# Large side items of TensorE cut in two pieces and issued from a queue with a share for each unit of scores

## What is computed

```python
x = x + 0.5 * ffn(layernorm(x))
x = x + attn(layernorm(x))
x = x + 0.5 * ffn(layernorm(x))
# attn: 16 heads of 16; k and q normalised per head, scaled by 256 ** -0.25
dot = where(causal, -inf, q @ k.T); out = softmax(dot) @ v; out @ Wo.T + bo
# ffn: base + shared low-rank + routed low-rank (6 experts of rank 16, 2 taken)
base_out = x @ base_W.T + base_b
shared_out = (x @ shared_A.T) @ shared_B.T
gate = softmax(x @ router_W.T + router_b); two largest, normalised, others 0
routed_out = sum over e of gate[e] * (x @ routed_A[e].T) @ routed_B[e].T
```

## Time and profile before

| | us |
|---|---|
| median of 3 runs | 1363.42 |
| lowest and highest run | 1358.17, 1364.6 |
| profiled execution | 1358.05 |
| its span, first to last instruction | 1356.3 |
| TensorE busy in it | 1164.8 |
| ScalarE busy in it | 1021.1 |
| VectorE busy in it | 458.1 |
| GpSimd busy in it | 232.9 |
| mean granted TensorE clock | 0.958 |

### The profile page before, as it was taken

The page is one execution under the profiler, slowest core; times in us unless marked ns, Lnnn a source line. Parts: engine busy times, 40 slices in busy tenths (PEclk is TensorE's granted clock), DMA queues, the critical chain, the costliest instruction groups (busy, mean ns, idle before and its releaser), DMA issues.

```text
span 1356.3 us, 23146 instructions
## 1 busy us (share of the span) xinstructions
PE 1164.8 (86%) x9076; PEld 382.2 (28%) x9076; DVE 458.1 (34%) x1164; ACT 1021.1 (75%) x1132; POOL 232.9 (17%) x377
## 2 busy tenths in 40 slices
PE   2636877889889998999989998999999999999984
PEld 2522432323323232232322222222222222121222
DVE  4655537356444533443234232122222011010114
ACT  2203555567677878788888997899999999999960
POOL 2223432222222122211022002102102001000000
PEclk9768898999999999999999999999999999999996
DMA  4011200300210021000200001100001100000000
GB/s 129 1 55 32 72 1 26 85 0 2 74 37 2 1 77 35 1 1 17 74 23 1 1 1 56 40 1 1 1 1 47 49 2 1 0 1 1 9 9 16
DMA packets 39673, 33.39 MB, mean 25 GB/s; under 512 B 8786, under 2 KB 39496, under 8 KB 39560
## 3 DMA queue, kind: packets, MB, share of 16 engines
q1 hardware_dynamic: 37360, 31.74, 8.0%
q10 hardware_dynamic: 2200, 0.12, 0.1%
HBM read 18.73 MB, written 12.85 MB: 23 GB/s over the span
## 4 chain that ended last, share of the span: by engine, by line
PE 61%; ACT 14%; DVE 11%; issue 8%; POOL 1%; DMA 1%; SPq 1%; ACTq 1%; DVEq 0%; POOLq 0%
PE ps L1088 56%; ACT ring L695 14%; PE ps L1127 2%; PE ps L1188 1%; DVE oT L1068 1%; DVE xnT L767 1%; DMA x<-in_x 1%; PE ps L1296 1%; DVE st L726 1%; SPq L527 1%; PE ps L1304 1%; PE ps L1147 1%; DVE xnT L765 1%; DVE area L747 1%; DVE att L1075 1%
## 5 line engine op out<-in xcount | busy, mean ns | idle before, releaser
L695 ACT ACTIVATE ring<-ps 128x1024 f32<-128x1024 f32 x1056 | 989.7, 1107 | 178.5 <-PE ps L1088 175.8
L1088 PE MATMUL ps<-ring,vf 128*17 128x512 f32 (+3 forms) x4608 | 566.0, 569 | 2.9 <-POOL ring L649 2.0
L1088 PE MATMUL ps<-queries,keys 50*128 50x512 f16 (+3 forms) x2304 | 380.4, 371 | 34.3 <-DMA queries<-shift_d 9.9
L1088 PEld LDWEIGHTS ps<-queries,keys 50*128 50x128 f16 x2304 | 93.5, 93 | 504.1 <-ACT ring L695 425.5
L649 POOL TENSOR_SCALAR_AFFINE_SELECT ring<-ring 128x256 f32<-128x256 f32 (+1 forms) x224 | 95.6, 443 | 434.0 <-ACT ring L695 432.9
L1088 PEld LDWEIGHTS ps<-ring,vf 128*17 128x17 f32 x4608 | 80.1, 96 | 173.5 <-issue 148.1
L765 DVE CAST xnT<-ps 128x512 f16<-128x512 f32 x50 | 34.5, 691 | 160.8 <-PE ps L1127 115.4
L1068 DVE COPY oT<-ps 128x512 f32<-128x512 f32 x32 | 22.1, 690 | 165.9 <-PE ps L1088 165.6
L899 DVE SCALAR_TENSOR_TENSOR x<-ps,power,x 128x512 f32<-128x512 f32 x32 | 24.0, 750 | 124.2 <-PE ps L1088 124.2
L461 POOL TENSOR_TENSOR sq<-area 128x512 f32<-128x512 f32 x32 | 33.7, 1052 | 184.4 <-DVE ss L904 89.7
L1088 PE MATMUL ps<-baseT,xnT 128*128 128x256 f16 x384 | 56.6, 287 | 8.1 <-DVE qT L932 2.7
(11 more groups left out here) (145 smaller groups left out, 703.7 us busy)
## 6 DMA issues: line engine op xcount, KB each, us to landing
parts_d<-split SPq DMA_DIRECT2D x32, 256.0 KB, 2.6
keys<-parts_d SPq DMA_DIRECT2D x96, 64.0 KB, 2.3
queries<-parts_d SPq DMA_DIRECT2D x192, 32.0 KB
x<-in_x SPq DMA_DIRECT2D x8, 512.0 KB, 3.9
out_x<-x SPq DMA_DIRECT2D x16, 256.0 KB, 2.2
queries<-shift_d SPq DMA_DIRECT2D x64, 4.0 KB
ring<-in_base_W SPq DMA_DIRECT2D x1, 256.0 KB, 4.6
ring<-in_Wq SPq DMA_DIRECT2D x1, 256.0 KB, 5.8
```

Source lines behind the costliest of these rows:

```text
L695: act.activation(probs[:, u % RING, :], bank(2 * (u % SLOTS), 2), ACTF.Exp, bias=0.0, scale=1.0).then_inc(exp_ok, 1)
L1088: return pe.matmul(o, lhsT, rhs, start=start, stop=stop, skip_group_check=True)
```

## The change

The side items of a unit are no longer issued at once. They are appended to a queue, and from it a unit issues items while the sum of their new weights (`PIECES`) stays within `SHARE`, 0.85. The first item of a unit is issued whatever it weighs, and steps that TensorE has no part in weigh 0. The queue is emptied whole 8 units and 3 units ahead of a chunk's end and at the last unit.

`inner`, `outer`, `qk`, `value` and `projout` become two entries in the queue: `("half", item)` for the first half of the matmuls, and the item itself for the second. Only the second signals that the bank is ready, and only the first waits for the bank. The other engines have no step named `half` and pass over it; they take their part at the second entry. When a `divide` is due and a first half is outstanding, its second half is issued ahead of it, since both use the same bank. At the start of the kernel both halves stand next to each other; the tail of chunk 7 isn't cut.

```diff
+
+PIECES = {"inner0": (2, 0.7), "inner1": (2, 0.7), "outer0": (2, 1.0), "outer1": (2, 1.0), "qk": (2, 0.75), "value": (2, 0.8), "projout": (2, 0.8),
+          "turn0": (1, 0.7), "turn1": (1, 0.7), "turn2": (1, 0.7), "turnin0": (1, 0.7), "turnin1": (1, 0.7), "turnout": (1, 0.7), "heads": (1, 0.7)}
+SHARE = 0.85
...
+def pieces(items):
+
+    for stage, n in items:
+        count, weight = PIECES.get(stage, (1, 0.0))
+        if count == 2:
+            yield weight, "half", (stage, n)
+        yield weight, stage, n
...
 def schedule():
     yield from startup()
-    for stage, n in together(prepare(0), front(0, 0, 1)):
+    for _, stage, n in pieces(together(prepare(0), front(0, 0, 1))):
         yield stage, n
...
-    values, groups, scored, split = [], [], set(), set()
+    values, groups, scored, split, queue, stage = [], [], set(), set(), deque(), None
...
         if groups and groups[0][0] <= u:
+            if stage == "half":
+
+                yield queue.popleft()[1:]
+                stage = None
             yield "divide", groups.pop(0)[1]
...
-        for stage, n in side[u]:
+        queue.extend(pieces(side[u]))
+        spent, flush = 0.0, u + 8 in UNIT0 or u + 3 in UNIT0 or u == NU - 1
+        while queue and (flush or not spent or spent + queue[0][0] <= SHARE):
+            w, stage, n = queue.popleft()
+            spent += w
             yield stage, n
...
+            def inner(K, f, c, halves=BOTH):
                 key = (f"inner{f}", c)
-                b = side_bank(K, key)
+                b = side_bank(K, key) if 0 in halves else bank(K.bank[key])
                 pe.wait_ge(K.w_ok, 1)
-                for a in range(2):
+                for a in halves:
                     pe.wait_ge(*K.done[f"turn{2 * f}", (c, a)])
-                for i in range(TC):
+                for i in (2 * a + k for a in halves for k in range(2)):
                     for ib in range(2):
                         m = mm_parts(b[:, i * NA:(i + 1) * NA], lambda s: xnT[2 * f][:, s, ib, i * P:(i + 1) * P], lambda s: aT[:, s, ib, :],
                                      i == 0 and ib == 0, i == TC - 1 and ib == 1)
-                m.then_inc(K.ready, 1)
+                if 1 in halves:
+                    m.then_inc(K.ready, 1)
...
-            def outer(K, f, c, a):
+            def outer(K, f, c, a, halves=BOTH):
                 key = (f"outer{f}", (c, a))
-                b = side_bank(K, key)
+                b = side_bank(K, key) if 0 in halves else bank(K.bank[key])
                 pe.wait_ge(K.w_ok, 3)
                 pe.wait_ge(*K.done[f"turnin{f}", c])
-                for i in range(2):
+                for i in halves:
                     t = slice((2 * a + i) * P, (2 * a + i + 1) * P)
                     o = b[:, i * D:(i + 1) * D]
                     for ib in range(2):
                         mm_parts(o, lambda s: xnT[2 * f][:, s, ib, t], lambda s: baseT[:, s, ib, :], i == 0 and ib == 0, False)
                     m = mm_parts(o, lambda s: hT[f][:, s, t], lambda s: bT[:, s, :], False, i == 1)
-                m.then_inc(K.ready, 1)
-
-            def project(K, n):
+                if 1 in halves:
+                    m.then_inc(K.ready, 1)
+
+            def project(K, n, halves=BOTH):
                 c, t = n // TC, slice(n % TC * P, (n % TC + 1) * P)
-                b = side_bank(K, ("qk", n))
+                b = side_bank(K, ("qk", n)) if 0 in halves else bank(K.bank["qk", n])
                 pe.wait_ge(K.w_ok, 5)
                 for i in range(2):
                     pe.wait_ge(*K.done["turn1", (c, i)])
-                for ib in range(2):
+                for ib in halves:
                     m = mm_parts(b, lambda s: xnT[1][:, s, ib, t], lambda s: qkT[:, s, ib, :], ib == 0, ib == 1)
-                m.then_inc(K.ready, 1)
-
-            def value(K, c, a):
-                b = side_bank(K, ("value", (c, a)))
+                if 1 in halves:
+                    m.then_inc(K.ready, 1)
+
+            def value(K, c, a, halves=BOTH):
+                b = side_bank(K, ("value", (c, a))) if 0 in halves else bank(K.bank["value", (c, a)])
                 pe.wait_ge(K.w_ok, 6)
                 for i in range(2):
                     pe.wait_ge(*K.done["turn1", (c, i)])
-                for i in range(2):
+                for i in halves:
                     for ib in range(2):
                         m = mm_parts(b[:, i * D:(i + 1) * D], lambda s: xnT[1][:, s, ib, (2 * a + i) * P:(2 * a + i + 1) * P],
                                      lambda s: vT[:, s, ib, :], i == 0 and ib == 0, i == 1 and ib == 1)
-                m.then_inc(K.ready, 1)
+                if 1 in halves:
+                    m.then_inc(K.ready, 1)
...
+            def project_out(c, a, halves):
+                key = ("projout", (c, a))
+                b = side_bank(main, key) if 0 in halves else bank(main.bank[key])
+                pe.wait_ge(*main.done["turnout", (c, a)])
+                for i in halves:
+                    for ib in range(2):
+                        m = mm_parts(b[:, i * D:(i + 1) * D], lambda s: xnT[2][:, s, ib, (2 * a + i) * P:(2 * a + i + 1) * P],
+                                     lambda s: woT[:, s, ib, :], i == 0 and ib == 0, i == 1 and ib == 1)
+                if 1 in halves:
+                    m.then_inc(main.ready, 1)
...
+            halved = None
             for stage, n in ORDER:
-                front_and_heads(main, stage, n)
+
+                if stage == "half":
+                    halved, halves = n, (0,)
+                    stage, n = n
+                else:
+                    halves = (1,) if (stage, n) == halved else BOTH
+                front_and_heads(main, stage, n, halves)
                 if stage == "scores":
                     scores(n)
...
-                    c, a = n
-                    b = side_bank(main, (stage, n))
-                    pe.wait_ge(*main.done["turnout", n])
-                    for i in range(2):
-                        for ib in range(2):
-                            m = mm_parts(b[:, i * D:(i + 1) * D], lambda s: xnT[2][:, s, ib, (2 * a + i) * P:(2 * a + i + 1) * P],
-                                         lambda s: woT[:, s, ib, :], i == 0 and ib == 0, i == 1 and ib == 1)
-                    m.then_inc(main.ready, 1)
+                    project_out(*n, halves)
```

More of the change, by code:

```diff
@@ L2 @@
 from concourse import mybir
+from collections import deque
 from contextlib import ExitStack
@@ L1128, in turn @@
                 m.then_inc(K.ready, 1)
-            def inner(K, f, c):
+            BOTH = (0, 1)
+            def inner(K, f, c, halves=BOTH):
                 key = (f"inner{f}", c)
-                b = side_bank(K, key)
+                b = side_bank(K, key) if 0 in halves else bank(K.bank[key])
                 pe.wait_ge(K.w_ok, 1)
-                for a in range(2):
+                for a in halves:
                     pe.wait_ge(*K.done[f"turn{2 * f}", (c, a)])
-                for i in range(TC):
+                for i in (2 * a + k for a in halves for k in range(2)):
                     for ib in range(2):
@@ L1189, in turn_heads, with front_and_heads @@
                 m.then_inc(K.ready, 1)
-            def front_and_heads(K, stage, n):
+            def front_and_heads(K, stage, n, halves=BOTH):
                 if stage == "weight":
@@ L1200, in front_and_heads @@
                 elif stage == "inner0":
-                    inner(K, 0, n)
+                    inner(K, 0, n, halves)
                 elif stage == "turnin0":
@@ L1204, in front_and_heads @@
                 elif stage == "outer0":
-                    outer(K, 0, *n)
+                    outer(K, 0, *n, halves=halves)
                 elif stage == "qk":
-                    project(K, n)
+                    project(K, n, halves)
                 elif stage == "value":
-                    value(K, *n)
+                    value(K, *n, halves)
                 elif stage == "heads":
                     turn_heads(K, *n)
+            def project_out(c, a, halves):
[8 more added lines that the diff above has]
+                    m.then_inc(main.ready, 1)
             pe.wait_ge(bnd, FLAG_STEPS)
@@ L1317, in _ @@
                 elif stage == "inner1":
-                    inner(main, 1, n)
+                    inner(main, 1, n, halves)
                 elif stage == "turnin1":
@@ L1321, in _ @@
                 elif stage == "outer1":
-                    outer(main, 1, *n)
+                    outer(main, 1, *n, halves)
 INPUTS = {
```

## The result

The kernel after takes 1389.46 us (median of 4 runs, 1388.80 to 1389.99), the kernel before 1361.75 beside it: a ratio of 1.0218, 95% interval 1.0193 to 1.0243. It is 2.2% slower. The forecast was 1348 us, 1327 to 1371, and faster.

The account below looks back on a forecast made before the run. ScalarE's wait for TensorE's scores, 175.8 us, was taken as the bound. Terms of -12.6, -1, -9, +6.6, -1, +2 and 0 gave -15.0 us: 1358.05 to 1343.0, then 5.4 up to a median of 1348, range 1327 to 1371.

Parts of the forecast that it names:

- (b): Chunks 2 to 6: 6 of 12 neighbour pairs sharing a unit are parted, saving bank wait and stall; 9 us gained.
- (a): Large items cut in two: 0.25 us gained an item in chunks 4 to 6, 0.1 in 2 and 3; 12.6 us.
- (c): Chunks 2 to 6: 11 more items start right behind another's end, each waiting 0.6 us for the bank; +6.6 us.
- a rival's reason: Rival of nothing measurable (1366 us, chance 0.20): side items share one bank, each holding it a unit longer.
- (d): Chunk 1: fewer items share a unit, more wait for the bank; net -1 us, ends -8 and +10.
- step (g): Work queued behind: VectorE and POOL steps come 0.3 to 0.4 units later in chunks 2 to 5, 2.2 in 1, unfelt.
- (e): Chunk 0: the flush at unit 12 makes a later but shorter burst, some 27 us; +2 us, ends -4 and +9.
- (f): Second pieces: their repeated semaphore waits are long satisfied and cost 0; at most 20 us for 95 pieces.
- The second rival: Chunks 0 and 1: the queue makes them a one-piece-a-unit chain, so slower by 11 us, 1374; chance 0.12.
- the 155 us: Mark of being right: ScalarE's wait for TensorE falls from 175.8 us to some 155.
- The wait of 2.25 us behind `heads` and `outer0`: Mark of being right: ScalarE's 2.25 us wait behind these two side items becomes about 1.
- (c)'s mark: Mark that the bank term is right: TensorE's waits for VectorE copies grow in number.

Follow-up runs that it names:

- e8: The changed kernel with items left whole and the queue only from chunk 2 on, chunks 0 and 1 in before's order; ratio to before .9992.
- e12: e8 with one unit left free behind each item's end; 1341.84 us, ratio to before .9865.
- e3: The changed kernel with the queue emptied in every unit of chunks 0 and 1, restoring before's order there; 1371.19 us, ratio to before 1.0091.
- e10: e3 with one unit left free behind each item's end from chunk 2 on; ratio to before .9924.
- e14: e12 with two free units instead of one behind an item's end from chunk 3 on; 1336.63 us, ratio to before .9826.
- e4: The kernel before, with every large item written as two entries next to each other, leaving only the repeated waits; ratio to before 1.0019.
- e1: The changed kernel with the queue and its flushes kept but no item cut; ratio to before 1.0027.

## Why the prediction was wrong

**What bounds the kernel** was read rightly: ScalarE waits for TensorE, chunks 0 and 1 are chains, and the single side bank is what pile-ups wait for. The sign of the cuts' term failed, and the gain under (b) did not come.

**(a) The cuts: -12.6 us; measured +8 to +13.5 us from chunk 2 on** (the table's columns). This is the step that failed. The flushes leave 92 of the 95 counted cuts parted. I took an item that stood alone, gave the first half its gain in full and returned half as a later stall. The runs show two costs that I had put at nothing. A cut costs TensorE .10 to .11 us: each half holds it for .76 us (300.51 to 301.27, 302.57 to 303.33), the whole for 1.40 (288.81 to 290.21), and so it is in all items from chunk 2 on. And it interrupts ScalarE's runs more often, 200 times instead of 135 in chunks 2 to 6, for .1 us each. A third is argued: a cut item fills two units, so the unit of slack in which ScalarE's lag was made good is gone. In chunk 2, at .4 us a cut, the first two don't cover the price, and its cause stays open in part. I let the bounds end at 0 though no row excluded a loss.

**(b) Pairs that shared a unit: -9 us.** e8 parts eight of the twelve and is at .9992, which leaves room for 3.5 us at most: where the queue puts them next door they wait for the bank again. The gain came only with a free unit between (e12, 17 us under e8 by the ratios, by the bank and this together).

**(c) The bank: +6.6 us.** Right, as far as the runs show it. I counted starts in the unit behind an end and without values (28 instead of 17) and priced each at .6 us; the row of 300.51 shows .59. Counted with those beside values and without `divide`, the free unit removes 36 such starts from e3 to e10 and 33 from e8 to e12 in chunks 2 to 6, for 23 and 17 us by the ratios, .6 and .5 us each. So the price held. What I missed is that 25 of them stood in before already, and that removing those was worth more than any cut. The Trainium skill (Perfetto Trace Analysis, Matmuls) asks for PSUM banks to be rotated so that emptying one overlaps the next matmuls; I had it as a rival's reason. The traces agree that the single bank costs: the waits in chunks 3 to 5 fell from 29.7 us (before) to 17.9 (e14) with more room between items. No run here has a second side bank; the kernel uses six banks for scores and one each for the values' sum and side work.

**(d) Chunk 1: -1 us, measured +7.3**, inside its ends. My counts of neighbours left out VectorE's order, which step (g) had dismissed; one place shows what it can cost. Timeline of after, chunk 1:

```profile
218.15 0.73 DVE L771 TENSOR_SCALAR area<-x,mv,rstd 128x256 f32<-128x256 f32 x2
218.79 0.56 DVE L936 TENSOR_SCALAR ss<-ss,epsq 128x64 f32<-128x64 f32 x2
...
222.86 0.69 DVE L791 TENSOR_TENSOR xnT<-ps,xnT 128x512 f16<-128x512 f32 x1
223.60 1.12 PE L1344 MATMUL ps<-ident,oT 128*128 128x128 f32 x4 [3.63 <-DVE xnT L791]
...
229.93 0.60 ACT L708 ACTIVATE vf<-ps 128x512 f32<-128x512 f32 x1 [11.10 <-PE ps L1112]
```

The steps of weight 0, scales and roots, leave the queue together from 218 us on; the copy of 222.86, which frees the bank for the divide's transpose, stands among them, TensorE waits 3.63 us, and ScalarE 11.10 us for the cut `value` behind that. How the 7.3 us are made up beyond this place isn't shown.

**(e) Chunk 0: +2 us, measured +6.6**, inside its ends. The burst began earlier than I had it and lasted longer. Timeline of after, and a window of it with ScalarE's busy time alone:

```profile
122.92 0.83 PE L1112 MATMUL ps<-vT,xnT 128*128 128x256 f16 x6
...
132.77 2.74 PE L1112 MATMUL ps<-vT,xnT 128*128 128x256 f16 x12 [5.10 <-DVE xnT L791]
...
155.67 1.16 PE L1174 MATMUL ps<-ident,area 128*113 128x128 f32 x4 [6.83 <-POOL area L475]
...
157.37 2.94 ACT L719 ACTIVATE ring<-ps 128x1024 f32<-128x1024 f32 x3
...
123.00:155.67 32.67, 4.19 (x7) 0.64 0.14 39
```

It runs from 122.92, not 126, to 155.67, so 32.8 us where I had 27 and before had 33.3. Taking the scores of nine units out of it shortened nothing: they had run in the waits of a chain through VectorE and GpSimd. TensorE is busy in 13.1 of the 32.7 us, in before's stretch in 21.5 of 33.3. The granted clock in it is .64, against .79, but that hides no gain: half of TensorE's busy time at the lower clock is 4.3 us here and 5.5 in before.

**(f) New waits: 0.** Right: e4 shows 0.4 to 4.9 us for 95 pieces. The 10 to 20 us by the Trainium skill (Advanced Engine Details and Errata, Network/Comms) did not come.

**Rivals and marks.** The second rival, slower by chunks 0 and 1, was nearest: they gave +14 of the +28 us (I had +19 at its ends), and it missed chunk 2 (+8.7), where the cuts cost most. Its mark, chunk 0 over 72 us, was just not reached (71.3). Of the marks of being right, the 155 us did not come, and no chunk shrank. The wait of 2.25 us behind `heads` and `outer0` did fall, to .57 and .39. Stalls of .4 to .8 us ahead of an exponential of chunks 2 to 6, which were to become smaller, are 38 in place of 17, with those over .8 still 59 against 56. TensorE's waits for VectorE there are 60 of 51.0 us in all, against 56 of 48.0, so (c)'s mark came, weakly.

## What to carry over

Where an item of work and its neighbour share one buffer, space them before cutting them: a free unit behind each whole item gave 1.3% (1.7% with two in the later chunks, of which only the first is shown), while no way of cutting gained over whole items in the same order, and the dearest cost 3.4%. Price a cut by all that it touches: the engine's own time for two pieces, each new break in the run of the engine that waits, the second slot, and what is queued behind the item in order. In the burst of chunk 0, scores taken out of a chain's waits shortened nothing.

## What the runs showed of the hardware

The granted clock went with part of the loss. In chunk 2, after and e3 have the same order; after took 127.5 us at .93, e3 124.7 at .96. Half of the time spent at the 1.2 GHz level is the most that it can have cost: 8.5 us in after's chunk 2 against 5.1 in e3's, and over all chunks 41.1 us against 25.5 before and 27.2 in e12, the faster kernel. But TensorE also waits at that level. Counted by its busy time there, the halves are 25.0 us after and 17.1 before, so 8 to 16 of the 32 us between the two profiled executions.

The longest such stretch of after, 20.5 us from 139.0 on, comes soon after the wait of 5.10 us ahead of 132.77, and TensorE is busy in only 9.7 us of it; so a chain that is lengthened can be slowed as well. Not every stretch follows a long wait: the last waits ahead of those from 128.8 and 221.0 are .8 and 1.0 us. What lowers the clock in chunk 2, where the orders were the same, stays open.

Runs of one program spread with it, too. Among the runs of before beside e12, the one at a mean clock of .960 took 1356.3 us and the one at .950 1365.28. e1's ten runs had a mean of .947, before beside them .957, so its 0.3% may be the clock's.
